# One layer of an early-fusion model: its elementwise passes and PE's order of work changed

## The reference

```python
C1, C2 = PHI * math.sqrt(2.0) * 51.85, math.pi / PHI
def qrt_damping(x):
    return jnp.sin(C1 * x) * jnp.exp(-(x * x) / PHI) + jnp.cos(C2 * x)
def ttt_filter(scores):
    mod9 = (jnp.abs(scores) * 1618.0).astype(jnp.int32) % 9
    chaos = (mod9 == 0) | (mod9 == 3) | (mod9 == 6)
    return scores * jnp.where(chaos, 1 / PHI, 1.0)
scores = ttt_filter(jnp.einsum('bhqd,bhkd->bhqk', q, k) / 8)     # 8 heads of 64
attn = jax.nn.softmax(scores, axis=-1)
attn = attn * qrt_damping(attn)
out = ctx(attn @ v) @ Wo + bo
```

## Time and profile before

| | us |
|---|---|
| median of 3 runs | 1701.41 (1700.09 to 1701.67) |
| the profiled execution | 1695.63 |
| its span, first to last instruction | 1693.9 |
| attn3, first call, from its first instruction to the next layer's | 219.3 (615.5 to 834.8) |
| attn3, second call | 219.2 (1424.5 to 1643.7) |
| PE, DVE, ACT, POOL busy over the span | 61%, 58%, 29%, 24% |

### The profile page before, as it was taken

How to read it: one execution, slowest core, us unless ns; L and a number is a source line. 1 busy time by engine, 2 the same in 40 slices (tenths; PEclk the granted TensorE clock), 3 DMA queues, 4 the chain that set the end, 5 groups by cost and what they waited for, 6 DMA issues and landing times. The chain is left out here.

```text
span 1693.9 us, 19367 instructions
## 1 busy us (share of the span) xinstructions
PE 1028.9 (61%) x6896; PEld 712.1 (42%) x6896; DVE 988.7 (58%) x2121; ACT 487.6 (29%) x1056; POOL 409.5 (24%) x378
## 2 busy tenths in 40 slices
PE   6455478674467875361755557867546788526176
PEld 3222336453245562151642233655434547215074
DVE  3469444475454628788546945447545461777854
ACT  0244112131132113436324411212213121442632
POOL 6024100102230004645202400010224000464420
PEclk9979577686585866555576967768758585755557
DMA  8100000000000000000000000000000000000000
GB/s 147 40 1 1 0 1 1 1 2 1 0 1 1 1 0 1 0 1 0 1 8 2 0 0 1 1 1 2 2 0 1 1 1 0 1 0 1 0 1 5
DMA packets 22615, 9.60 MB, mean 6 GB/s; under 512 B 20261, under 2 KB 21994, under 8 KB 22420
## 3 DMA queue, kind: packets, MB, share of 16 engines
q1 hardware_dynamic: 20980, 8.20, 2.5%
q0 software_dynamic: 1536, 0.12, 0.1%
HBM read 7.98 MB, written 0.34 MB: 5 GB/s over the span
## 5 line engine op out<-in xcount | busy, mean ns | idle before, releaser
L2409 PE MATMUL banks<-ident,attn_frac 82*82 82x82 f32 x256 | 41.5, 343 | 145.3 <-DVE attn_frac L2624 110.0
L609 PE MATMUL banks<-ident,xn 82*64 82x82 f32 x112 | 21.1, 344 | 173.8 <-DVE xn L585 173.8
L597 POOL TENSOR_TENSOR ffn_sums<-ffn_sums,neg_half 82x4 f32<-82x4 f32 (+1 forms) x36 | 50.8, 1426 | 210.0 <-DVE ffn_sums L582 210.0
L2409 PEld LDWEIGHTS banks<-ident,attn_frac 82*82 82x82 f32 x256 | 34.5, 189 | 153.4 <-DVE attn_frac L2624 135.4
L910 DVE TENSOR_TENSOR_SCAN state<-decay,drive 128x164 f32<-128x164 f32 x128 | 93.5, 770 | 1.8 <-POOL drive L703 1.8
L2343 POOL TENSOR_TENSOR attn_mag<-attn_mag,attn_low 82x656 f32<-82x656 f32 x32 | 58.5, 1828 | 145.3 <-DVE attn_low L2580 145.3
L609 PEld LDWEIGHTS banks<-ident,xn 82*64 82x64 f32 x112 | 12.8, 159 | 180.5 <-DVE xn L585 180.5
L703 POOL TENSOR_TENSOR drive<-spread_b,dtx 128x328 f32<-128x328 f32 x64 | 56.5, 886 | 94.6 <-DVE state L910 51.5
L2426 PE MATMUL banks<-attn_vals,attn_aT 82*82 82x64 f32 x512 | 78.2, 346 | 0.0
L2496 ACT ACTIVATE attn_z<-attn_z,attn_peak 82x164 f32<-82x164 f32 x128 | 53.4, 418 | 76.6 <-DVE attn_peak L2598 76.5
L2426 PEld LDWEIGHTS banks<-attn_vals,attn_aT 82*82 82x82 f32 x512 | 74.5, 261 | 1.9
(11 more groups left out here) (540 smaller groups left out, 2925.4 us busy)
## 6 DMA issues: line engine op xcount, KB each, us to landing
n_sel_bc<-c_sel_bc_dram SPq DMA_DIRECT2D x1, 1536.0 KB, 10.5
image<-x_dram SPq DMA_DIRECT2D x18, 48.0 KB, 2.7
n_w<-L_ffn_w_dram SPq DMA_DIRECT2D x2, 320.0 KB
f_Wd<-L_ffn_Wd_dram SPq DMA_DIRECT2D x2, 256.0 KB
f_W<-L_ffn_W_dram SPq DMA_DIRECT2D x2, 256.0 KB
n_sel_expert<-c_sel_expert_dram SPq DMA_DIRECT2D x1, 510.0 KB, 11.9
n_w<-L_ffn_w_dram SPq DMA_DIRECT2D x1, 340.0 KB
out_dram<-h SPq DMA_DIRECT2D x2, 164.0 KB
```

The costliest lines, as they stand in the source:

```text
L597: pool.tensor_tensor(sums, sums, half, ALU.pow).then_inc(rstd_ready, 1)
L2409: last = pe.transpose(ps[4 + par][0:TP, (2 * c + t) * TP:(2 * c + t + 1) * TP], frac[:, i, par, c, t * TP:(t + 1) * TP], w.ident[0:TP, 0:TP])
```

## The change

The filter becomes one-sided: floor(y/3) is taken as the nearest whole number to y/3 - 1/2 (ACT `thirds`, DVE stage 0), y - 1 is formed (DVE stage 2 in group 0, ACT `less_one` in group 1), "3 floor(y/3) is at most y - 1" gives 1 or 0 (DVE stage 1), and the larger of that and 1/PHI times the score is the result (DVE stage 3). GpSimd keeps three constants and the reciprocal roots; its remainder is gone, its squares go to ACT (group 0) and DVE (group 1), its rest of group 0 and its products to DVE. On ACT `thirds` stands between the sine and the cosine of a step, `less_one` behind the cosine. PE issues scores once ahead of its last loop and then between `turn_weights(j)` and `weigh(j - 1)`. The lists of semaphores and GpSimd's removed loops are cut short here.

```diff
--- before.py
+++ after.py
@@ -2307,14 +2307,15 @@
         z, frac, damp = (sb(n, [TP, STEPS] + step) for n in ("z", "frac", "damp"))
         cosine = sb("cosine", [TP, 2] + step)
         peak, total = sb("peak", [TP, STEPS, 4]), sb("total", [TP, STEPS, 4])
-        half_pi = sb("half_pi", [TP, 1])
+        half_pi, minus_half, minus_one = (sb(n, [TP, 1]) for n in ("half_pi", "minus_half", "minus_one"))
...
@@ -2336,42 +2337,11 @@
         def _(pool):
             pool.memset(half_pi[:, :], HALF_PI).then_inc(const_ready, 1)
             pool.wait_ge(const_ready, 1)
+            pool.memset(minus_half[:, :], -0.5).then_inc(const_ready, 1)
+            pool.wait_ge(const_ready, 2)
+            pool.memset(minus_one[:, :], -1.0).then_inc(const_ready, 1)
+            pool.wait_ge(const_ready, 3)
             roots(pool, w, [s for s, in per_group(sums)], var_ready, rstd_ready, 0)
-
-            def remainder(j):
-                pool.wait_ge(three_ready, j + 1)
-                pool.tensor_tensor(flat(mag, j % 2), flat(mag, j % 2), flat(low, j % 2), ALU.subtract
-                                   ).then_inc(frac_ready, 1)
-
-            def square(j):
-                i = j % STEPS
-                pool.wait_ge(z_ready, j + 1)
-                pool.tensor_tensor(flat(damp, i), flat(z, i), flat(z, i), ALU.mult).then_inc(square_ready, 1)
-
-            def product(j):
-                i = j % STEPS
-                pool.wait_ge(sin_ready, j + 1)
-                pool.wait_ge(damp_ready, j + 1)
-                pool.tensor_tensor(flat(damp, i), flat(frac, i), flat(damp, i), ALU.mult).then_inc(prod_ready, 1)
-
-            for t in range(STEPS + 3):
-                if t < STEPS:
-                    remainder(t)
-                if t >= 3:
-                    square(t - 3)
-                    pool.wait_ge(turns_ready, t - 2)
-                    pool.tensor_tensor(flat(frac, t - 3), flat(z, t - 3), flat(frac, t - 3), ALU.subtract
-                                       ).then_inc(rest_ready, 1)
...
@@ -2456,11 +2426,13 @@
             pe.wait_ge(v_ready, NT)
             pe.wait_ge(q_ready, 4 * GROUPS)
             pe.wait_ge(k_ready, 4 * GROUPS)
+            if STEPS < ALL:
+                scores(STEPS)
             for j in range(ALL + 1):
-                if j + STEPS < ALL:
-                    scores(j + STEPS)
                 if j < ALL:
                     turn_weights(j)
+                if j + STEPS + 1 < ALL:
+                    scores(j + STEPS + 1)
                 if j:
                     weigh(j - 1)
 
@@ -2480,13 +2452,29 @@
 
             for i in range(4):
                 keys(i)
-            act.wait_ge(const_ready, 1)
+            act.wait_ge(const_ready, 3)
 
             def size(j):
                 act.wait_ge(s_ps, j + 1)
                 if j >= 2:
-                    act.wait_ge(held_ready, j - 1)
+                    act.wait_ge(kept_ready, j - 1)
                 act.activation(mag[:, j % 2, :, :, :], scores_of(j), ACT.Abs, scale=1618.0 / 8.0).then_inc(mag_ready, 1)
+
+            def thirds(j):
+                act.wait_ge(mag_ready, j + 1)
+                if j >= 2:
+                    act.wait_ge(filtered, j - 1)
+                act.activation(flat(low, j % 2), flat(mag, j % 2), ACT.Identity, scale=1.0 / 3.0,
+                               bias=minus_half[:, 0:1]).then_inc(third_ready, 1)
+
+            def less_one(j):
+                act.activation(flat(mag, j % 2), flat(mag, j % 2), ACT.Identity, bias=minus_one[:, 0:1]
+                               ).then_inc(less_ready, 1)
+
+            def square(j):
+                i = j % STEPS
+                act.wait_ge(z_ready, j + 1)
+                act.activation(flat(damp, i), flat(z, i), ACT.Square).then_inc(square_ready, 1)
 
             def exponentials(j):
                 i = j % STEPS
@@ -2503,10 +2491,13 @@
                 act.activation(flat(damp, i), flat(damp, i), ACT.Exp, scale=-1.0 / (TURN * TURN * PHI)
                                ).then_inc(damp_ready, 1)
 
-            def waves(j):
+            def sines(j):
                 i = j % STEPS
                 act.wait_ge(rest_ready, j + 1)
                 act.activation(flat(frac, i), flat(frac, i), ACT.Sin, scale=BELOW_2PI).then_inc(sin_ready, 1)
+
+            def cosines(j):
+                i = j % STEPS
                 if j >= 2:
                     act.wait_ge(sum_ready, j - 1)
                 act.activation(flat(cosine, j % 2), flat(z, i), ACT.Sin, scale=-C2 / TURN, bias=half_pi[:, 0:1]
@@ -2519,27 +2510,36 @@
                 act.activation(aT[:, j % 2, :, :], w.banks[0:TP, 4:6, 0:4 * TP], ACT.Copy).then_inc(aT_ready, 1)
 
             act.preload_act_table(ACT.Exp)
-            for t in range(STEPS + 4):
+            for t in range(STEPS + 5):
                 if t < STEPS:
                     size(t)
                     if t < 4:
                         for i in range(4 + t, 4 * GROUPS, 4):
                             keys(i)
+                    thirds(t)
                 if 1 <= t <= STEPS:
                     exponentials(t - 1)
                 if 4 <= t < STEPS:
                     for i in range(2 * (t - 4), NT, 8):
                         values(i)
                         values(i + 1)
-                if t >= 4:
-                    damping(t - 4)
+                if t >= 5:
+                    damping(t - 5)
+                if 4 <= t < STEPS + 4:
+                    square(t - 4)
             for g in range(1, GROUPS + 1):
                 act.preload_act_table(ACT.Sin)
                 for t in range(STEPS + 3):
                     if g < GROUPS and 2 <= t < STEPS + 2:
                         size(g * STEPS + t - 2)
                     if t < STEPS:
-                        waves((g - 1) * STEPS + t)
+                        sines((g - 1) * STEPS + t)
+                    if g < GROUPS and 2 <= t < STEPS + 2:
+                        thirds(g * STEPS + t - 2)
+                    if t < STEPS:
+                        cosines((g - 1) * STEPS + t)
+                    if g < GROUPS and 2 <= t < STEPS + 2:
+                        less_one(g * STEPS + t - 2)
                     if t >= 3:
                         copy_turned((g - 1) * STEPS + t - 3)
                 if g < GROUPS:
@@ -2570,26 +2570,23 @@
 
                 g, i = j // STEPS, j % STEPS
                 y, lo, f = flat(mag, j % 2), flat(low, j % 2), flat(z, i)
-                y4, lo4, f4 = mag[:, j % 2, :, :, :], low[:, j % 2, :, :, :], z[:, i, :, :, :]
+                lo4, f4 = low[:, j % 2, :, :, :], z[:, i, :, :, :]
                 heads = f4.rearrange("p a c n -> p (a c) n")
                 if s == 0:
-                    dve.wait_ge(mag_ready, j + 1)
-                    dve.tensor_scalar(lo, y, 1.0 / 3.0, MAGIC, ALU.mult, ALU.add).then_inc(low_ready, 1)
+                    dve.wait_ge(third_ready, j + 1)
+                    dve.tensor_scalar(lo, lo, MAGIC, -MAGIC, ALU.add, ALU.add).then_inc(floor_ready, 1)
+                elif s == 2:
+                    dve.wait_ge(third_ready, j + 1)
+                    dve.tensor_scalar(y, y, -1.0, None, ALU.add).then_inc(less_ready, 1)
                 elif s == 1:
-                    dve.wait_ge(low_ready, j + 1)
-                    dve.tensor_scalar(lo, lo, -MAGIC, 3.0, ALU.add, ALU.mult).then_inc(three_ready, 1)
-                elif s == 2:
-                    dve.wait_ge(frac_ready, j + 1)
-                    dve.scalar_tensor_tensor(out=lo4, in0=y4, scalar=0.0, in1=scores_of(j), op0=ALU.is_ge,
-                                             op1=ALU.mult).then_inc(above_ready, 1)
-                elif s == 9:
-                    dve.wait_ge(above_ready, j + 1)
-                    dve.scalar_tensor_tensor(out=lo, in0=y, scalar=1.0, in1=lo, op0=ALU.is_lt,
-                                             op1=ALU.mult).then_inc(held_ready, 1)
+                    dve.wait_ge(floor_ready, j + 1)
+                    dve.wait_ge(less_ready, j + 1)
+                    dve.scalar_tensor_tensor(out=lo, in0=lo, scalar=3.0, in1=y, op0=ALU.mult, op1=ALU.is_le
+                                             ).then_inc(kept_ready, 1)
                 elif s == 3:
-                    dve.wait_ge(held_ready, j + 1)
-                    dve.scalar_tensor_tensor(out=f4, in0=lo4, scalar=1.0 / PHI - 1.0, in1=scores_of(j), op0=ALU.mult,
-                                             op1=ALU.add).then_inc(filtered, 1)
+                    dve.wait_ge(kept_ready, j + 1)
+                    dve.scalar_tensor_tensor(out=f4, in0=lo4, scalar=1.0 / PHI, in1=scores_of(j), op0=ALU.max,
+                                             op1=ALU.mult).then_inc(filtered, 1)
                 elif s == 4:
                     dve.wait_ge(filtered, j + 1)
                     dve.tensor_reduce(peak[:, i, :], heads, X, ALU.max).then_inc(peak_ready, 1)
@@ -2606,12 +2603,21 @@
                 elif s == 10:
```

(67 more changed lines are left out.)

## The result

The kernel after the change takes **1637.62 us** (median of 4 runs, 1633.99 to 1638.96), the kernel before beside it 1701.11 us (1700.09 to 1701.67). The ratio is 0.9624, with a 95% interval of 0.9607 to 0.9641. The forecast was 1643.8 us, with a range of 1633 to 1655.

A forecast was written before the change was run, and what follows sets the result against it. Bounds by attn3 stage: A DVE with GpSimd, B that loop and PE with ACT nearly alike, C GpSimd's square holding DVE, D PE. Gains 13.4, 7.0, 5.0, 3.4: 28.8 a call, 57.6 off 1701.41 gives 1643.8 us; range 1633 to 1655.

The forecast's parts named there:

- The two loops of B: In Stage B before: PE with ACT, 8.4 us with bias, about 7.7 without; DVE with GpSimd, nearly alike.
- The prices: Costs per 656-element pass: DVE two-source 0.83 us, one-source 0.49; ACT 0.71 to 0.83; Identity with bias taken as 0.83.
- Stage A: In attn3, group 0 filtered and exponentiated: step 7.30 us, first sine at 690.0, gain 13.4 us a call.
- Stage B: In attn3, group 1 filtered, group 0 weighed: step 6.95 us, stage 53.0, gain 7.0 us a call.
- Stage C: In attn3, group 1 exponentiated: DVE sets a step of 2.75 us, stage 25.5, gain 5.0 us a call.
- Stage D: In attn3, group 1 weighed: 3.4 us to the first transposes instead of 6.8, gain 3.4 us a call.
- PE's 32 us stand: In Stage D, the 32 us from the first transposes to the end stay unchanged.
- (a): Rival: the clock rises in Stage B and Stage D, 34 us less over both calls, 1610 us; chance 4%.
- (b): Rival: DVE becomes the bound, its passes costing 0.83 to 0.87 us; 1644 to 1656, say 1652 us; chance 14%.
- (c): Rival: Identity is not in the sine's table set, so loads add 31 us a call in Stage B; 1706 us; 3%.
- (d): Rival: the loop closes elsewhere, through sum and cosine buffers, and Stage B keeps its length; 1658 us; chance 3%.
- what a measurement can tell: For the whole kernel: about 0.2%, 3.4 us, is what a measurement can tell from no change.

The follow-up runs named there:

- the second experiment: PE's new order alone (scores ahead of the weighing) put into the kernel before; 1700.42 us, ratio 1.0003.
- the fastest one: Kernel after with the copy of turned weights first in the sine loop, and damping and square ahead of the exponentials; 1604.07 us, ratio 0.9425.

## Why the prediction was right

**What bounds the kernel.** The two loops of B were seen, but only PE's was worked out, as 8.4 and 7.7. The other one, DVE with GpSimd at 7.67, was the one that set the stage (the second experiment). That did not hurt the forecast, which was made from the new loop forward and not from the old one's gain. It did mislead the expectation for the new order in the old kernel. One reference was a slip as well: the 48.6 us that DVE waits for the remainder are not in the row named there but in this one of before's page:

```profile
L2583 DVE SCALAR_TENSOR_TENSOR attn_low<-attn_mag,banks 82x656 f32<-82x656 f32 x32 | 26.7, 833 | 48.6 <-POOL attn_mag L2343 48.6
```

**The prices.** The largest unknown was Identity with a bias: 0.74 to 0.93, taken as 0.83. The product and the comparison on DVE were taken as 0.83. The page's groups and the filter's tile in the trace of after:

```profile
L2619 DVE TENSOR_TENSOR attn_damp<-attn_frac,attn_damp 82x656 f32<-82x656 f32 x32 | 26.6, 832 | 14.5 <-ACT attn_frac L2497 14.5
```

```profile
L2467 ACT ACTIVATE attn_low<-attn_mag,attn_minus_half x32: 829/832/842, 629.1 to 1512.9; 82x656 f32<-82x656 f32 x32
L2584 DVE SCALAR_TENSOR_TENSOR attn_low<-attn_low,attn_mag x32: 827/834/840, 631.3 to 1514.9; 82x656 f32<-82x656 f32 x32
...
L2471 ACT ACTIVATE attn_mag<-attn_mag,attn_minus_one x16: 825/830/833, 692.6 to 1513.6; 82x656 f32<-82x656 f32 x16
```

All are right to 0.01 us, and no DVE pass of these lines is stretched any more.

**Stage A.** Step 7.30 forecast, 7.28 measured; ACT's wait 1.83 forecast, 1.80 measured. The times of the exponentials were given on before's clock; with the 2.55 us added by which `attn3` starts earlier in after, the eight groups and the first sine all come 0.1 to 0.4 us before the times forecast, the sine at 689.7 instead of 690.0. These 0.3 us are the difference between 13.4 and 13.75.

**Stage B.** Step 6.95 forecast, 6.96 measured; PE's part 2.81 and 2.82; the stage 53.0 and 53.15. The experiments show three parts of that loop one by one: an ACT pass of 0.73 (one taken out, 0.73 less), the weighing of 2.43 (put back, the step is 9.5, 2.55 more), and the copy that waits behind the sines (moved ahead, DVE's queue becomes the bound). PE's busy share was overestimated, 74% against 68%.

**Stage C.** 25.5 forecast, 25.50 measured; the step 2.75 and 2.73.

**Stage D.** 3.4 us to the first transposes forecast, 3.42 measured. The 32 us behind them were held fixed and came out 31.65. That is the 0.36 by which D's gain of 3.4 was undersized. All of it lies between the first transposes and the next: 3.32 us (769.24 to 772.56) in after, 3.69 (800.83 to 804.52) in before, and 3.70 with the product back on GpSimd. In before PE waited there for ACT's copy:

```profile
804.52 1.29 PE L2409 MATMUL banks<-ident,attn_frac 82*82 82x82 f32 x8 [0.17 <-ACT attn_aT L2519]
```

That copy stood in ACT's queue behind a cosine that had waited 2.77 us for DVE's sum, 2.21 us long beside GpSimd. So the term "PE's 32 us stand" left out one more place where the chain through GpSimd was late.

**The rivals.** (a) The clock stayed at 0.50 in B and D. The Trainium skill (TensorE: Matmul & The Clock Gate, "What's actually happening") would have a busy PE rise to 2.4 GHz; the trace of after, with PE at 68% of B and 94% of D's stretch, disagrees as that of before did. This rival's price for D was too high: it took 4.0 us a step, while PE's first transposes in before come 3.98 and 3.30 apart in turn, 3.64 in the mean, so that D would have given about 8 us and not 10. (b) DVE's passes are 0.75 apart and not 0.83. In B it waits 1.85 us a step for y/3 and so is not the bound; in A it and ACT wait for each other in turn, as forecast; in C it is the bound, at the rate forecast. (c) No table load stands beside Identity, neither in B (707.28 to 714.24 has none) nor in A. By the Trainium skill (ScalarE: Activation LUTs, "Table sets: the hidden batching unit") identity is a filler in every set, and the trace agrees: 48 Identity passes, and none but the loads of before. (d) B's loop did close where it was said to.

**The total.** `attn3` gave 58.8 us where 57.6 were forecast. The medians differ by 63.5. The forecast's miss of 6.2 us is made up of this 1.2, of 0.3 by which before's median of four runs is lower than the one used, and of 4.7 that lie outside `attn3` and are not explained. The layers outside are the same instructions in all twelve kernels profiled here, yet `attn3` starts between 613.0 and 618.5 us, and 588.1 to 596.5 us lie between the calls. Over the eleven changed kernels the median's gain differs from twice the gain of the stages by -2.5 (the remainder on DVE) to +5.8 us (the product on GpSimd), with +4.3 for the fastest one. So the size is right to 1.2 us in the part that the change touches. The 3.4 us that the prediction took for what a measurement can tell was too little for such comparisons.

## What to carry to other kernels

Before pricing an edit to a loop that crosses engines, write down every loop through the stage with its length, the one that looks second too: here a reordering worth 15 us a call was worth nothing until the other edits had shortened the loop beside it, and those alone would have lengthened the stage by 8.5. In an engine's hand-written queue, put what others wait for first, and work that needs no answer into the place where the engine waits; two such moves gave another 16.3 us a call. To ask which loop is late, move one pass from one engine to the other: the sign of the result answers, and its size against the pass's own says how far.

## What the runs showed of the hardware

- A GpSimd pass stretches one-source DVE passes as well as two-source ones: 0.50 to 1.24 us (floor, with the product on GpSimd) and 0.49 to 1.12 (L2571, with only the remainder moved). The GpSimd pass is stretched itself, from 1.57 to 2.18 us. The prediction had named two-source passes only, though the one-source L2613 with a longest pass of 1.75 us stood in its own.
- The stages A to D repeat from call to call to 0.03 us in before and after, and to 0.09 in the experiments; the stretch ahead of A varies more, from 13.42 to 13.69. They also repeat from kernel to kernel where a stage was not edited (A 59.42 to 59.44 in six kernels; D 38.31 to 38.45 in five, and 38.23 to 38.45 with the three in which only the copy moved ahead in it). The untouched layers vary by 5 to 8 us from one profiled kernel to the next.
